# Node degrees of a graph layer from one-hot products with an iota row in SBUF, in place of a second sort and searched key runs

## The chip, the cores and the metric

The kernel runs on one core of a Trainium2 chip. The metric is the device time of one execution in microseconds, the median over the runs shown; lower is better.

## The reference

A block over 16 images of 32x32 pixels and 128 channels: a layer norm and three convolutions with a residual, then a layer norm and a graph-attention router over the 16384 pixels (nodes) with four experts, with a residual again.

```python
h = (x_flat @ W_gat).reshape(M, HEADS, NUM_EXPERTS)          # M = 16384 here, edge_index in [0, 32768)
src, dst = concat(edge_index[0], loops), concat(edge_index[1], loops)      # 524288 edges and loops
e = leaky_relu(a_src[src] + a_dst[dst])
ee = exp(e - segment_max(e, dst)[dst])                        # per destination node
alpha = ee / (segment_sum(ee, dst)[dst] + 1e-16)
agg = segment_sum(h[src] * alpha[:, :, None], dst)            # + b_gat, layer norm, top 2 of 4 experts
out = sum over experts of g * (gelu(x @ W1[ei] + b1[ei]) @ W2[ei] + b2[ei])
```

The edges' numbers run to twice the number of nodes: an edge whose destination lies beyond the last node is dropped, and one whose source lies beyond it reads the last node. So three kinds of edge matter: dropped ones (half), those that read the last node's row, and real ones (a quarter, some 131072), whose source rows have to be fetched one by one.

## The kernel before, in words

Stages. From 0 to some 630 us PE, ACT and DVE run the convolutions and norms, and DVE in between sorts the edges. Each edge is one f32 key that holds destination and source (destination above 14 bits of source); real edges have keys below REAL_END, last-row edges lie between it and VALID_END. The 128x4096 keys stand in SBUF (KA). `sort_row` splits each partition's row so that the small keys come first; the first LROW = 1152 columns of all partitions form list 0, which `sort_keys(0)` sorts over partitions and columns. The next 1152 columns, picked by `pick_rest` (L1285 to L1299), are list 1; what is left is "the rest".

Rows. PE transposes list 0, ACT copies it out (L975), `sources` (L1423) masks the source numbers, and POOL fetches the node rows by indirect DMA: `gather_rows` (L511, the DMA at L519) makes nine gathers of 128 rows a trip, SP stores each trip's rows to `payload`. There are 54 early trips (EARLY_TRIPS), then a loop of catch-up trips whose number is read from a register (`catch_up_trips`, L530 to L534), the rest keys one by one (`fetch_rest`, L546 to L550), four gathers for overlong nodes (L598), and then the main loop: 32 node groups, each with row trips spread over them (61 in all, 540 gathers of L519 in that stage) and gathers of 24 slots per node from `payload` (L616). DVE does the attention of a node group when its slots have landed. PE and ACT run the 32 chunks of the experts (`experts`, L734; 12 layers and 4 groups of transposes a chunk) beside all of this, 16 of them before ACT's exponentials of the last row's start values (init), the others in the main loop.

Starts of the nodes' runs. To know where each node's edges begin in the sorted lists, `find_starts(a)` takes each 64th key as a pivot, compares them with an iota row on DVE (L1471: one-hots of the high and the low part, f32 in, bf16 out, 6 batches of 3 columns per list), PE multiplies the one-hots into a histogram (L773), and POOL gathers key runs of 192 around the starts (`gather_windows`, L566: 32 gathers for list 0 after trip 5, 16 for list 1 after trip 42). DVE counts in each run the keys below each limit (L1523, L1524). For this the sorted keys are stored to DRAM by SP and ACT (`store_keys`), and list 1 has to be sorted fully (`sort_keys(1)`).

Order. Each engine's order is the program's own: POOL's is trips 0 to 4, windows of list 0, trips 5 to 41, windows of list 1, trips 42 to 53, catch-up, rest, main loop. Buffers of two trips of rows alternate (L516 waits for the store of the trip before the last).

```python
for t in range(COLS):                                          # L517, nine a trip
    pool.indirect_dma_start(row_buf[h][:, t, :], None, node_dram, ...)
```

## Time and profile before

| | us |
|---|---|
| median of 3 runs (lowest, highest) | 2872.55 (2868.71, 2882.48) |
| span of the profiled execution | 2297.5 |
| what lies around the span, by the median | 575.05 |
| DVE busy | 1594.7 |
| POOL busy | 1212.5 |
| PE busy | 1086.1 |
| ACT busy | 762.8 |

For the profiled execution only its span is on record, no time of its own. The span runs from the first to the last instruction or transfer. Busy times are of the execution that was profiled; a DMA that an engine issues is not counted as busy, with one exception: POOL's indirect gathers are shown as instructions of POOL, with the time that POOL spends on them. "Issue" stands for idle time that nothing in the profile ends.

### The profile page before, as it was taken

How to read it: one execution, taken by the hardware profiler on the slowest of the kernel's cores; microseconds unless marked ns; L12 is line 12 of the kernel's file. 1: busy time of each engine (PE TensorE's matmuls, PEld its weight loads, DVE VectorE, ACT ScalarE, POOL GpSimd, SP SyncE). 2: the span in 40 equal slices, each digit the busy share in tenths (PEclk: the TensorE clock that was granted, in tenths of full speed). 3: DMA queues.
4: the chain of work that ended last, by engine and by line, in shares of the span. 5: the costliest groups of instructions: out<-in, count | busy, mean ns of one | idle time of the engine just before them, and what ended most of it. 6: DMA issues, size and time to landing. Idle time of an engine off the chain costs nothing. (4 is left out here: it accounts for less than half of the span.)

```text
span 2297.5 us, 16425 instructions
## 1 busy us (share of the span) xinstructions
PE 1086.1 (47%) x4821; PEld 479.8 (21%) x4821; DVE 1594.7 (69%) x3100; ACT 762.8 (33%) x1260; POOL 1212.5 (53%) x1233
## 2 busy tenths in 40 slices
PE   3897878778678887000700102433342425333330
PEld 1233343334533333000300001111111112111110
DVE  6999999995726999999209504364758384747658
ACT  4664846535345554000300002222232324222221
POOL 2000000000066777777777764777777777777771
PEclk8898878787589999555855556766676768676665
DMA  8202031021454322111221611344453535363543
GB/s 297 115 1 74 1 8 38 1 8 39 47 57 110 79 71 71 14 15 29 48 41 29 43 16 41 98 144 121 121 176 85 165 92 176 72 187 73 169 113 100
DMA packets 185735, 182.76 MB, mean 80 GB/s; under 512 B 81580, under 2 KB 164462, under 8 KB 176046
## 3 DMA queue, kind: packets, MB, share of 16 engines
q1 hardware_dynamic: 99262, 88.84, 14.4%
q0 software_dynamic: 43936, 47.85, 12.4%
q10 hardware_dynamic: 42448, 45.04, 6.4%
q8 instruction: 38, 0.62, 0.1%
q14 instruction: 51, 0.42, 0.1%
HBM read 105.23 MB, written 76.40 MB: 79 GB/s over the span
## 5 line engine op out<-in xcount | busy, mean ns | idle before, releaser
L519 POOL DMA_INDIRECT KC<-node_dram,KB x1026 | 1018.4, 993 | 938.8 <-DMA node_dram<-node_out 626.3
L740 PE MATMUL hidden_out<-XT,W 128*128 128x512 f32 x512 | 291.3, 675 | 540.8 <-ACT ARENA_A L956 539.9
L745 PE MATMUL hidden_out<-ARENA_A,W 128*128 128x512 f32 x512 | 264.7, 642 | 24.9 <-ACT ARENA_A L956 24.9
L956 ACT ACTIVATE ARENA_A<-hidden_out,b1c 128x512 f32<-128x512 f32 x256 | 174.2, 687 | 294.5 <-PE hidden_out L740 293.9
L740 PEld LDWEIGHTS hidden_out<-XT,W 128*128 128x128 f32 x512 | 97.3, 211 | 689.5 <-ACT ARENA_A L956 570.1
L1523 DVE TENSOR_TENSOR KB<-XG,MB 128x3072 bf16<-128x3072 f32 x20 | 67.1, 3354 | 163.5 <-DMA XG<-rest_dram,win_i 100.7
L1649 DVE TENSOR_SCALAR KB<-MB 128x16 f32<-128x16 f32 (+1 forms) x33 | 5.7, 172 | 238.3 <-DMA KC<-payload,slot_idx 126.8
L1800 DVE SCALAR_TENSOR_TENSOR XG<-XT,KB,XG 128x128 f32<-128x128 f32 x512 | 144.3, 347 | 14.9 <-DMA XT<-ye_dram 11.2
L959 ACT ACTIVATE ARENA_A<-hidden_out,b2c 128x512 f32<-128x512 f32 x128 | 87.9, 687 | 185.5 <-PE hidden_out L745 185.5
L1026 ACT ACTIVATE TA<-KB 128x400 f32<-128x400 f32 x32 | 16.2, 507 | 373.3 <-DVE KB L1656 373.2
L745 PEld LDWEIGHTS hidden_out<-ARENA_A,W 128*128 128x128 f32 x512 | 98.3, 207 | 182.4 <-ACT ARENA_A L956 103.1
L1201 DVE TENSOR_TENSOR KC<-KA 128x576 f32<-128x576 f32 (+2 forms) x126 | 108.2, 859 | 3.2 <-DVE shift L1095 0.2
L752 PE MATMUL Z<-ident,ARENA_A 128*128 128x128 f32 x512 | 76.5, 296 | 64.9 <-ACT ARENA_D L967 39.9
L1202 DVE TENSOR_TENSOR KC<-KA 128x576 f32<-128x576 f32 (+2 forms) x126 | 107.0, 849 | 0.0
L1201 DVE TENSOR_TENSOR KA<-KC 128x576 f32<-128x576 f32 (+2 forms) x112 | 94.2, 841 | 2.8 <-DVE shift L1085 0.2
L773 PE MATMUL MB<-KC 128*128 128x128 bf16 x36 | 4.9, 307 | 188.5 <-DVE KC L1471 188.5
L1202 DVE TENSOR_TENSOR KA<-KC 128x576 f32<-128x576 f32 (+2 forms) x112 | 93.5, 834 | 0.0
L1524 DVE TENSOR_REDUCE KC<-KB 128x16 f32<-128x3072 bf16 x24 | 80.5, 3354 | 0.8
L616 POOL DMA_INDIRECT KC<-payload,slot_idx x64 | 61.2, 956 | 34.8 <-issue 34.8
L752 PEld LDWEIGHTS Z<-ident,ARENA_A 128*128 128x128 f32 x512 | 58.3, 148 | 100.8 <-ACT ARENA_A L959 51.4
L967 ACT ACTIVATE ARENA_D<-Z 128x512 f32<-128x512 f32 x128 | 70.0, 592 | 25.9 <-PE Z L752 25.9
L1661 DVE TENSOR_TENSOR KC<-KC,TA 128x1600 f32<-128x1600 f32 x16 | 29.1, 1821 | 69.5 <-ACT TA L1026 69.5
(401 smaller groups left out, 2232.0 us busy)
## 6 DMA issues: line engine op xcount, KB each, us to landing
ye_dram<-ARENA_D ACTq DMA_DIRECT2D x32, 1024.0 KB, 4.0
XT<-ye_dram SPq DMA_DIRECT2D x32, 1024.0 KB, 13.5
KC<-node_dram,KB POOLq DMA_INDIRECT x1026
payload<-XT SPq DMA_DIRECT2D x1, 11520.0 KB
payload<-KC SPq DMA_DIRECT2D x115, 90.0 KB, 1.8
XG<-x_dram SPq DMA_DIRECT2D x32, 256.0 KB, 11.3
out_dram<-XG ACTq DMA_DIRECT2D x32, 256.0 KB, 3.4
KA<-in_L_ffn_edge_index_dram SPq DMA_DIRECT2D x1, 2048.0 KB, 9.0
```

The lines of the kernel that those rows point to most:

```text
L519: pool.indirect_dma_start(row_buf[h][:, t, :], None, node_dram, bass.IndirectOffsetOnAxis(ap=KB[:, col:col + 1].bitcast(I32), axis=0)).the ...
L740: last = pe.matmul(PF[i % 2][:, :], W1[:, m // 2, (m % 2) * P:(m % 2) * P + P], XT[:, n * CHUNK:(n + 1) * CHUNK], start=True, stop=True)
L745: last = pe.matmul(PF[i % 2][:, :], W2[:, 2 * m + kk, :], HH[:, 2 * m + kk, :], start=kk == 0, stop=kk == 1)
L752: last = pe.transpose(Z[:, t % 2, x_ * C:(x_ + 1) * C], HH[:, 2 * x_, t * P:(t + 1) * P], ident[:, :])
L956: act.activation(HH[:, m, :], PF[i % 2][:, :], ACT.Gelu, bias=b1c[:, m:m + 1]).then_inc(S["hid_out"], 1)
L959: act.activation(HH[:, 2 * m, :], PF[i % 2][:, :], ACT.Identity, bias=b2c[:, m:m + 1]).then_inc(S["hid_out"], 1)
L967: act.activation(YE[n % 2][:, t, :], Z[:, t % 2, :], ACT.Copy).then_inc(S["exp_out"], 1)
L1201: tt(part(dst, at, 0), part(src, at, 0), part(src, at, 1), ALU.max if d else ALU.min)
L1202: last = tt(part(dst, at, 1), part(src, at, 0), part(src, at, 1), ALU.min if d else ALU.max)
L1523: window_link(tt(below, bc(windows[n % WIN_BUFS], 1, shape), bc(limits, 3, shape), ALU.is_lt))
L1524: window_link(red(found[:, :, j:j + PAIR_J].rearrange("p c j -> p j c"), below, AX.X, ALU.add))
L1800: last = stt(tail_x[j][:, t, :], expert[:, t, x_ * C:(x_ + 1) * C], gate[:, at * TPC + t, x_:x_ + 1], tail_x[j][:, t, :], ALU.mult, ALU.add)
```

## The change

The sorted lists are no longer searched. Instead, for every key of list 0 and list 1 DVE makes two one-hot rows, one of the destination's low seven bits (128 wide) and one of its high bits (256 wide for list 0: the lower half are real nodes, the upper half last-row edges; 128 wide for list 1, the upper half alone). PE multiplies them, 128 keys at a time, into one 128x256 count in PSUM (`H`), which then is the degrees of the nodes. So list 1 doesn't have to be sorted. `drop_counted` takes its last-row edges out once they are to be counted; real keys in it, were there any, stay in the rest, which is now all columns behind list 0.

- Gone: pivots, `find_starts`, `count_keys`, `gather_windows` on POOL, `store_keys` on SP and ACT, `sort_keys(1)`, the boundary products on PE.
- `split_digits(a)` (four DVE instructions a list) writes each key's two digits as bf16, each twice, beside each other. `node_iota` is an iota row of 256 in bf16, in SBUF. `one_hots(a)`: 144 batches of HOT = 8 key columns; a batch is two tensor_tensor (is_equal) into one of two buffers, and from the third batch on it waits until PE has read the buffer (`hot_used`).
- `count_nodes` on PE: eight matmuls per batch, 128x256 (list 0) or 128x128 (list 1). Three batches stand ahead of each of the 16 slots (12 layers, 4 transposes) of the FFN chunks 0 to 2 and 5 to 7 (HOT_SLOTS).
- The starts come from the degrees by two products (with a triangular matrix and with ones) and a scan. ACT loads the node rows after chunk 1 and stores the rest after chunk 7.

```diff
+HOT = 8
+HOT_BATCHES = LROW // HOT
-FIRST_TRIPS = 5
-MID_TRIPS = 42
 EARLY_TRIPS = 54
-REST = ROW - LISTS * LROW
+REST = ROW - LROW
+HOT_SLOTS = (3, 3, 3, 0, 0, 3, 3, 3)
+STORE_REST_AFTER = 7
...
-            for trip in range(FIRST_TRIPS):
-                gather_rows(trip)
-            gather_windows(0)
-            for trip in range(FIRST_TRIPS, MID_TRIPS):
-                gather_rows(trip)
-            gather_windows(1)
-            for trip in range(MID_TRIPS, EARLY_TRIPS):
+            for trip in range(EARLY_TRIPS):
                 gather_rows(trip)
...
+            def count_nodes(count):
+                for n in islice(batches, count):
+                    real = n < HOT_BATCHES
+                    pe.wait_ge(S["hot_ready"], n + 1)
+                    for t in range(HOT):
+                        last = pe.matmul(H if real else H[:, P:], hot_p[n % 2][:, t, :],
+                                         hot_l[n % 2][:, t, 0 if real else P:],
+                                         start=n == 0 and t == 0, stop=n == LISTS * HOT_BATCHES - 1 and t == HOT - 1,
+                                         skip_group_check=True)
+                    last.then_inc(S["hot_used"], 1)
...
+            for n, beside in enumerate(HOT_SLOTS):
+                experts(n, beside)
             pe.wait_ge(S["degree_ready"], 1)
+            pe.matmul(TA[0][:, 0:P], before[:, :], degree_t[:, :], start=True, stop=True)
+            pe.matmul(TA[0][:, P:2 * P], ones[:, :], degree_t[:, :], start=True, stop=True).then_inc(S["starts_summed"], 1)
+            experts(len(HOT_SLOTS))
...
-            sorting = [chain(split_keys(), sort_row(), sort_keys(0)), chain(pick_rest(), sort_keys(1))]
+            sorting = [chain(split_keys(), sort_row(), sort_keys()), pick_rest()]
...
+            def split_digits(a):
+                keys = half(KA, a).bitcast(I32)
+                link(ts(digit_i, keys, SRC_BITS, P - 1, ALU.logical_shift_right, ALU.bitwise_and))
+                link(cp(digits_p, bc(digit_i, 2, [P, LROW, 2])))
+                link(ts(digit_i, keys, SRC_BITS + 7, None, ALU.logical_shift_right))
+                link(ts(digits_l, bc(digit_i, 2, [P, LROW, 2]), float(-(KEY_BIAS // P)), None, ALU.add))
+
+            def one_hots(a):
+                pairs = lambda ap: ap.rearrange("p t (n e) -> p t n e", e=2)
+                for b in range(HOT_BATCHES):
+                    n = a * HOT_BATCHES + b
+                    if n >= 2:
+                        dve.wait_ge(S["hot_used"], n - 1)
+                    cols = slice(b * HOT, (b + 1) * HOT)
+                    for hot, digits, low, high in ((hot_p, digits_p, 0, P), (hot_l, digits_l, (0, P)[a], 2 * P)):
+                        shape = [P, HOT, (high - low) // 2, 2]
+                        last = tt(pairs(hot[n % 2][:, :, low:high]),
+                                  bc(node_iota[:, low:high].rearrange("p (n e) -> p n e", e=2), 1, shape),
+                                  bc(digits[:, cols, :], 2, shape), ALU.is_equal)
+                    last.then_inc(S["hot_ready"], 1)
...
+            split_digits(0)
+            one_hots(0)
             sort_steps(ROW, 1)
+            split_digits(1)
+            drop_counted()
+            one_hots(1)
```

How the instructions move, on the engines that wait or are waited for. POOL before, between the first row gathers and the catch-up trips (L519 row gathers, L566 window gathers, L377 the read of the windows' rounds, L368 that of the catch-up trips):

```order
L519 DMA KC<-node_dram,KB 128x20 x45
L377 TENSOR_LOAD counts_i
L377 ISA x2
...
L566 DMA XG<-keys_dram,win_i 128x192 x8
...
L519 DMA KC<-node_dram,KB 128x20 x333
...
L566 DMA XG<-rest_dram,win_i 128x192 x8
...
L519 DMA KC<-node_dram,KB 128x20 x108
L368 TENSOR_LOAD counts_i
```

and the same place now (L470 is the row gather, L485 that of the catch-up trip, L340 the read of its number):

```order
L470 DMA KC<-node_dram,KB 128x20 x486
L340 TENSOR_LOAD counts_i
L340 ISA x2
L512 UNCONDITIONAL_BRANCH
L512 ISA
L481 ISA
L481 COPY src_buf<-KB 128x9
L482 REGISTER_ALU
L485 DMA KC<-node_dram,src_buf 128x20 x9
```

The 48 window gathers and both reads of a round count between row gathers are gone; 486 row gathers follow each other.

DVE after the sort of list 0, before (L1451 to L1456 make the pivots' digits, L1471 the one-hots, L1523 and L1524 count in a window):

```order
L1456 CAST piv_f<-piv_i 128x18
L1423 TENSOR_SCALAR KB<-KB 128x1152
L1460 COPY MB<-thresholds 128x256
L1471 TENSOR_TENSOR KC<-iota_f,piv_f 128x768
L1471 TENSOR_TENSOR KC<-iota_f,piv_f 128x384
...
L1523 TENSOR_TENSOR KB<-XG,MB 128x3072
L1514 ISA
L1524 TENSOR_REDUCE KC<-KB 128x2x8
```

and now (L1322 masks the sources, L1343 to L1346 are the digits, L1359 the one-hots):

```order
L1322 TENSOR_SCALAR KB<-KB 128x1152
L1376 CAST node_iota<-iota_f 128x256
L1343 TENSOR_SCALAR KC<-KA 128x1152
L1344 CAST KB<-KC 128x2304
L1345 TENSOR_SCALAR KC<-KA 128x1152
L1346 TENSOR_SCALAR KB<-KC 128x2304
L1359 TENSOR_TENSOR KC<-node_iota,KB 128x1024
L1359 TENSOR_TENSOR KC<-node_iota,KB 128x2048
L1359 TENSOR_TENSOR ARENA_Y<-node_iota,KB 128x1024
L1359 TENSOR_TENSOR ARENA_Y<-node_iota,KB 128x2048
```

288 such instructions stand for list 0 where 12 stood, and 288 (128x1024 and 128x8x128) for list 1 behind `pick_rest`. On PE the products stand between the FFN's layers; before, they stood in one block ahead of them (L740 and L745 were the layers, L773 the products, L778 to L785 the offsets):

```order
L773 MATMUL MB<-KC 128x128 x6
L773 MATMUL MB<-XG 128x128 x6
L778 MATMUL TA<-hist_tot,before 128x2
L779 MATMUL TA<-hist_tot,ones 128x1
L785 MATMUL TA<-ident,max_deg 1x128
L740 MATMUL hidden_out<-XT,W 128x512 x3
L745 MATMUL hidden_out<-ARENA_A,W 128x512 x2
```

and now (L672 the products, L685 and L690 the layers):

```order
L672 MATMUL MB<-KC 128x256 x8
L672 MATMUL MB<-ARENA_Y 128x256 x8
L672 MATMUL MB<-KC 128x256 x8
L685 MATMUL hidden_out<-XT,W 128x512
L672 MATMUL MB<-ARENA_Y 128x256 x8
L672 MATMUL MB<-KC 128x256 x8
L672 MATMUL MB<-ARENA_Y 128x256 x8
L685 MATMUL hidden_out<-XT,W 128x512
```

So a layer of these chunks stands behind three batches of products, and with them behind DVE's one-hots.

## Rows read from the trace of the kernel before

**Rows 1.** the page's head: the span, then busy us (share of span) and instructions of engines
```profile
span 2297.5 us, 16425 instructions
...
PE 1086.1 (47%) x4821; PEld 479.8 (21%) x4821; DVE 1594.7 (69%) x3100; ACT 762.8 (33%) x1260; POOL 1212.5 (53%) x1233
```

**Rows 2.** POOL's groups: xcount | busy us, mean ns of one | idle us before, releasers
```profile
L519 POOL DMA_INDIRECT KC<-node_dram,KB x1026 | 1018.4, 993 | 938.8 <-DMA node_dram<-node_out 626.3 <-issue 312.2 <-DVE ARENA_Y L1666 0.3
...
L566 POOL DMA_INDIRECT XG<-keys_dram,win_i x24 | 22.8, 948 | 18.3 <-DVEq L1525 11.3 <-issue 7.0
```

**Rows 3.** busy time of all engines (instructions) in two stretches, granted clock, DMA share, GB/s
```profile
639.00:1361.00 722.00, 290.36 (x845) 126.92 (x845) 477.68 (x668) 169.14 (x260) 547.75 (x535) 0.71 0.27 49
1407.00:2228.00 821.00, 317.38 (x764) 135.53 (x764) 481.93 (x1033) 245.12 (x350) 622.62 (x651) 0.69 0.44 124
```

**Rows 4.** POOL's timeline at five places: start us, duration us, instruction [idle before <-releaser]
```profile
639.13 2.18 POOL L519 DMA_INDIRECT KC<-node_dram,KB  x1 [626.29 <-DMA node_dram<-node_out]
...
737.70 0.95 POOL L566 DMA_INDIRECT XG<-keys_dram,win_i  x1 [11.25 <-DVEq L1525]
...
1360.11 0.21 POOL L530 COPY src_buf<-KB 128x9 int32 x1
...
1377.54 0.59 POOL L546 DMA_DIRECT2D rest_key<-rest_dram  x1 [5.44 <-issue]
...
2226.90 0.95 POOL L519 DMA_INDIRECT KC<-node_dram,KB  x1 [0.30 <-issue]
```

**Rows 5.** DVE's timeline where the catch-up counts and the first rest key are
```profile
1306.04 0.14 DVE L1615 CAST counts_i<-counts_f 1x1 int32<-1x1 f32 x1
...
1380.47 0.15 DVE L1682 TENSOR_SCALAR rest_idx<-rest_key 128x1 int32<-128x1 int32 x1 [60.17 <-DMA rest_key<-rest_dram]
```

**Rows 6.** POOL's groups by form, 697 to 823 us, beside the windows' counting on DVE
```profile
L519 POOL DMA_INDIRECT KC<-node_dram,KB x61 | 57.7, 946 | 18.6 <-issue 18.6
```

**Rows 7.** POOL's groups by form, 840 to 1090 us, beside the second list's sort
```profile
L519 POOL DMA_INDIRECT KC<-node_dram,KB x175 | 197.4, 1128 | 53.3 <-issue 53.3
```

**Rows 8.** DVE's and POOL's timelines at 1314 us, long two-input operations
```profile
1314.67 2.29 DVE L1629 TENSOR_TENSOR KB<-last_row,KC 128x2048 f32<-128x2048 f32 x1
...
1315.76 2.02 POOL L519 DMA_INDIRECT KC<-node_dram,KB  x1 [0.31 <-issue]
```

**Rows 9.** the old one-hots: durations by form of their line; DVE's, then POOL's timeline
```profile
L1471 DVE TENSOR_TENSOR KC<-iota_f,piv_f x12: 548/749/958, 632.2 to 1099.0; 128x768 bf16<-128x768 f32 x6, 128x384 bf16<-128x384 f32 x6
...
1095.44 1.42 DVE L1471 TENSOR_TENSOR KC<-iota_f,piv_f 128x768 bf16<-128x768 f32 x2
...
1096.18 1.03 POOL L519 DMA_INDIRECT KC<-node_dram,KB  x1 [0.30 <-issue]
1097.51 1.04 POOL L519 DMA_INDIRECT KC<-node_dram,KB  x1 [0.30 <-issue]
```

**Rows 10.** a bf16 reduction (the page's groups) and a one-source operation (timeline)
```profile
L1524 DVE TENSOR_REDUCE KC<-KB 128x16 f32<-128x3072 bf16 x24 | 80.5, 3354 | 0.8
...
1267.05 1.09 DVE L1438 TENSOR_SCALAR KB<-KA 128x1792 f32<-128x1792 f32 x1
```

**Rows 11.** POOL's group, 823.8 to 838 us, beside pick_rest; DVE's timeline, start and end of halving
```profile
L519 POOL DMA_INDIRECT KC<-node_dram,KB x11 | 11.1, 1013 | 3.4 <-issue 3.4
...
823.83 0.69 DVE L1201 TENSOR_TENSOR KB<-KA 128x512 f32<-128x512 f32 x1
824.44 0.68 DVE L1202 TENSOR_TENSOR KB<-KA 128x512 f32<-128x512 f32 x1
...
858.90 0.29 DVE L1296 COPY KA<-KB 128x256 f32<-128x256 f32 x1
```

**Rows 12.** PE's timeline at the old one-hots; PE in two stretches (busy us, granted clock, DMA)
```profile
633.80 0.80 PE L773 MATMUL MB<-KC 128*128 128x128 bf16 x6 [3.70 <-DVE KC L1471]
...
632.00:642.00 10.00, 4.90 (x36) 0.50 1.77 35
700.00:850.00 150.00, 134.57 (x385) 1.00 0.35 87
```

More of the change, by code:

```diff
@@ L733, in _, with experts @@
             last_chunk()
-            def experts(n):
+            batches = iter(range(LISTS * HOT_BATCHES))
+            def count_nodes(count):
[8 more added lines that the diff above has]
+                    last.then_inc(S["hot_used"], 1)
+            def experts(n, beside=0):
                 done = n * len(LAYERS)
                 for i, (layer, m) in enumerate(LAYERS):
+                    count_nodes(beside)
                     if layer == 1:
@@ L749, in experts @@
                 for t in range(TPC):
+                    count_nodes(beside)
                     pe.wait_ge(S["exp_out"], n * TPC + t + 1)
@@ L802, in _ @@
             pe.transpose(PO[0:1, 3 * P:], hist_tot[:, 1:2], ident[:, :]).then_inc(S["max_deg_t"], 1)
+            for n in range(len(HOT_SLOTS) + 1, FIRST_CHUNKS):
+                experts(n)
             for n in range(FIRST_CHUNKS, FFN_CHUNKS):
@@ L1295, in pick_rest @@
                 assert n == PICK
[L1296 to L1309 removed]
+                link(cp(a[:, 0:2 * n], b[:, 0:2 * n]))
             def row_steps(keys, other, spare):
@@ L1333, in quadrant_step, with sort_keys @@
                 link(stt(keys, copy, -1.0, frm, ALU.mult, ALU.min))
-            def sort_keys(which):
-                keys, copy, other = (half(k, which) for k in (KA, KB, KC))
+            def sort_keys():
+                keys, copy, other = (half(k, 0) for k in (KA, KB, KC))
                 def times_sign(col, frm=keys):
                     link(ts(keys, frm, signs[:, col:col + 1], None, ALU.mult))
-                if which:
-                    yield from row_steps(keys, other, copy)
                 for m in range(1, LEVELS + 1):
                     if m <= 4:
-                        if m > 1 or which:
+                        if m > 1:
                             times_sign(m - 1, other)
@@ L1556, in _ @@
             measure_rest()
+            dve.sem_inc(S["max_deg_ready"], 1)
             dve.wait_ge(S["nodes_in"], 48)
```

313 lines of the change are left out of this document (62 added, 251 removed).

## The prediction

> **What bounds the kernel now.** All sums are made against the profiled execution. Its span is 2297.5 us [rows 1]; the median of the runs is 2872.55 us, so 575.05 us lie around the span, and I carry them over unchanged. A shift of 0.5% is 14.4 us, about what a measurement of this kernel can tell from no change.
>
> I read the busy shares first. They mislead: DVE is busy 69% and POOL only 53% [rows 1]. The groups of POOL's instructions correct this: 1026 row gathers (L519), 993 ns each, with 312.2 us of idle time before them called issue [rows 2]. That is 0.30 us before each gather, and nothing in the trace ends it; so I count 0.95 + 0.30 = 1.25 us per gather as POOL's own time. Counted so, POOL is full: from 1407 to 2228 us it runs 651 instructions in 821 us, and 651 x 1.25 = 814 [rows 3]. POOL's timeline shows the fixed points: the first gather at 639.13 us waits for the conv stage, the 54 early trips end at 1360.11 us, the rest key follows at 1377.54, and the last row gather comes at 2226.90 [rows 4]. Behind that about 70 us of attention are left. The whole span from 639 us on is therefore POOL's queue, and the change acts on its part from 639 to 1360 us.
>
> Everything else has slack there. DVE has the catch-up counts by 1306.2 us, and POOL reads them only at 1360; DVE then idles 60.17 us for the rest key [rows 5]. So DVE, PE and ACT may end up to some 55 us later at no cost; what counts is what DVE does to POOL's gathers.
>
> **What holds a gather.** While DVE runs the window counts (one SBUF input, or a reduction), gathers take 946 ns [rows 6]. Beside the sort they take 1128 ns [rows 7], 1.43 us with the issue time. The long operations tell why: beside a 2.29 us tensor_tensor with two SBUF inputs, a gather takes 2.02 us [rows 8]. It ends some 0.8 us after the next operation has begun. So I read: a gather that starts inside a DVE operation with two SBUF inputs waits until this operation ends, then takes some 0.8 us, and the next is issued 0.30 us later. A gather is released about 1.12 us after the one before at the soonest, and only where an operation ends.
>
> The window between 639.13 and 1360.11 us then adds up: 720.98 us hold 54 x 9 = 486 row gathers and 32 + 16 window gathers, 534 x 1.25 = 668; 11.25 us of waiting for the first windows' count [rows 4]; and 41 us of holding, 31 of them beside the second list's sort (175 x (1.128 - 0.946) = 32, [rows 6, 7]).
>
> **The change part by part.**
> (1) Removed from POOL: 48 window gathers, 60 us, and the wait of 11.25 us. Catch-up, rest and main loop keep their instructions.
> (2) Removed from DVE: the windows' counting and the second list's sort; on POOL this is worth the holding beside the sort, about 31 us. I leave about 14 us of holding in place: pick_rest's halving and the setup of the last row stay, and the measuring of the rest grows from 1792 to 2944 columns.
> (3) Added on DVE: one-hots, 144 batches of two tensor_tensor for each list. Before, one-hots had f32 inputs, and 768 and 384 elements took 0.95 and 0.55 us, one element per cycle [rows 9]. Now inputs and output are bf16 in SBUF, in adjacent pairs. No row shows such an operation. The bounds are one element per cycle, as the bf16 reduction has (3072 in 3.354 us [rows 10]), and two, as a one-source operation has (1792 in 1.094 us [rows 10]). I take two: two f32 inputs pass at one element per cycle, and half as many bytes per element are read now. This is an estimate. A batch of list 0 (1024 and 2048 elements) is then 0.60 + 1.14 = 1.74 us, 251 us in all; of list 1 (1024 and 1024) 1.21 us, 174 us in all.
>
> The Trainium skill ("VectorE: DVE Perf Modes", section "The perf-mode tier table (the rule you actually need)") gives a bf16 tensor_tensor in SBUF two results per cycle, 1224 ns for 2048. Taken as spacing, its figure makes a batch of list 0 1.84 us, and the sum below would be 14 us more, about no change. In the rows a duration stands 0.08 us over the spacing (0.69 and 0.61 [rows 11]), so I keep 1.74; the page is not shown by any row here.
>
> (4) What this does to POOL. With list 0 a gather released at the end of the 2048-wide operation is ready 1.12 us later, after the 1024-wide one has ended (0.60), and waits for the next end of a wide one: one gather per batch, 1.74 us. The row for this pattern is the old pair of 768 and 384: one gather per pair, 1.04 + 0.30 = 1.34 us, the pair's own period [rows 9]. So 144 x (1.74 - 1.25) = **+71 us**. The bounds are 0 (nothing is held) and +85: 6% over the lock, as the sort's 1.43 us stands over two of its 576-wide operations (0.61 us of spacing at 512 [rows 11], 64 columns more at 1.04 ns, so 1.35 for two).
> With list 1 the operations end every 0.60 us, as the 512-wide ones of pick_rest do. Beside those a gather takes 1.013 + 0.31 = 1.32 us [rows 11]. So 144 x 0.07 = **+10 us**; bounds 0 and +56 (first rival).
> (5) The sum: 486 x 1.2515 = 608.2, the first gather 1.2 longer, +71, +10, +14: 704.4 us. The early trips end at 639.1 + 704.4 = 1343.5 instead of 1360.1: **17 us earlier, 2856 us**.
> (6) What must stay hidden. DVE: one-hots from 641 us, list 0 done at 892; pick_rest's halving took 823.83 to 859.2, 35 us [rows 11], digits and dropping 8 more: 936; list 1 at 1.25 us a batch until 1116; starts and counts some 27 us, so by 1145, 200 us before POOL asks. PE: six 128-column matmuls took 0.80 us at clock 0.50 [rows 12]; eight of 256 columns are then at most 2.13 us at that level and 1.07 at clock 1.00, which the FFN stretch had [rows 12]. It ran 385 instructions in 150 us, 48 a chunk, so 18.7 us a chunk and 1.17 a slot. Three batches and a slot are 3 x 1.07 + 1.17 = 4.4 us, less than DVE's 5.2: PE keeps up. Eight chunks remain after the lists, 150 us: ACT reaches its init exponentials at about 1270 and DVE ends that work by 1300, 43 us before POOL's early end. The removed key stores of SP and ACT free nothing on POOL: only the removed window gathers read them. The larger store of the rest (1.5 MB) goes out at about 1110, 250 us before its reader.
>
> **The rivals.**
> *A, slower: list 1 holds for three operations.* Two operations last 1.21 us, and an undisturbed gather comes back after 1.25. If it then finds the third operation running by more than some 0.05 us, it waits for its end: 1.82 us instead of 1.25. In 178 us 98 gathers fit, 98 x 0.57 = +56 instead of +10: **2902 us**. It decides against the change once the holding in list 1 passes 27 us. For it: the sort's mean of 1.43 lies above two of its operations (1.35), so some of its gathers took three. Against: the 512-wide rows, of nearly the same spacing, show 1.32 in the mean.
> *B: one element per cycle.* Batches of 3.34 and 2.27 us: lists done at 641 + 481 + 44 + 327 = 1493, init after eight chunks at 1655. The rest key then waits until 1668 instead of 1377: **3163 us**. For it speaks the bf16 reduction.
> *C: 16-bit inputs don't hold gathers.* POOL is through at 1262, and the rest key waits for DVE's init at 1298: 79 us earlier, **2793 us**. For it: gathers beside one-input and reduction rows aren't held; against: the two inputs are still both in SBUF.
> *D: PE stays at the low level (1.2 GHz).* Three batches and a slot: 3 x 2.13 + 2.3 = 8.7 us in list 0, 5.5 in list 1: lists done at 1368, init at 1540, **about 3010 us**. Against: the stretch that had PE busy 90% was granted 1.00 [rows 12].
> *E: DVE is held as POOL is.* Each operation would wait for a whole gather: 3.64 and 3.11 us a batch, lists done at 1656, **about 3340 us**. Against: DVE's 512-wide operations kept a spacing of 0.61 us beside gathers [rows 11]. The Trainium skill ("SBUF — State Buffer", section "Who interferes with whom") says that a DVE instruction with two SBUF inputs contends with a GpSimd instruction that reads SBUF, and that the one that issues first holds the ports while the other fully blocks. The trace agrees for the gather (2.02 us [rows 8]), not for DVE.
> That the change did not do what it says (real keys left to the rest loop) I give nothing: that loop ran one trip before [rows 4], so the second list held no real key.
>
> **How the numbers follow.** The forecast of 2856 with its spread of some 15 us: 0.56, of which 0.32 lies below 2858 and 0.24 within 14 us of no change. A: 0.20 (0.03 of it within). C: 0.10. B and D: 0.06 each. E: 0.02. Faster by over 0.5%: 0.32 + 0.10 = 0.42; within: 0.27; slower: 0.17 + 0.14 = 0.31. The likeliest case's own range is 2835 to 2875. The range takes in C (2793) and A (2902) with their spread, 2790 to 2910, and leaves out B, D and E, 0.14, and some of the tails.
>
> **What would show it.** Right: no POOL wait between 639 and the catch-up trip; L470 gathers at 1.74 us spacing while L1359 runs 2048-wide, at 1.25 to 1.32 in list 1; the rest key at about 1361; DVE idle before it by 40 us or more. Wrong: L1359 1024-wide over 0.75 us (B); gathers at 0.95 throughout (C); PE's clock at 0.50 from 641 to 892, and DVE waiting for hot_used (D); gathers of 1.5 us in list 1 (A); POOL idle before the rest key by more than 6 us, which would mean that the FFN chunks have become the bound.

## The result, and the profile after

| us | before | with the change |
|---|---|---|
| median of five runs | 2874.22 | 2947.64 |
| lowest, highest | 2868.71, 2882.48 | 2932.92, 2953.82 (four runs) |
| ratio, with its 95% interval | | 1.0242 (1.0211 to 1.0272) |

The change makes the kernel slower by 2.4%, some 70 us. Of its five runs, the one that was profiled took 3088.51 us, 4.6% above the next; it counts in the median but not in the range and the ratio, and the rows of the change below are from another profiled execution, of 2948.21 us. Beside it the kernel before was profiled a second time, in an execution of 2879.56 us. The heads of both pages, the change first:

```profile
span 2946.6 us, 20726 instructions
...
PE 1376.0 (47%) x7034; PEld 655.7 (22%) x7034; DVE 1610.9 (55%) x3152; ACT 765.7 (26%) x1260; POOL 1214.0 (41%) x1184
```

```profile
span 2877.6 us, 16425 instructions
...
PE 1230.1 (43%) x4821; PEld 511.6 (18%) x4821; DVE 1589.6 (55%) x3100; ACT 765.8 (27%) x1260; POOL 1196.5 (42%) x1233
```

These two heads already contradict the frame of the prediction. The time of these executions is the span plus 1.6 and 2.0 us (2948.21 - 2946.6, 2879.56 - 2877.6), and in all the other profiled runs with a time 1.6 to 2.3 us. Nothing of 575 us lies around the span. The execution of [rows 1], with a span of 2297.5 us, was one that none of the timed runs resembles: in the second profile of before the missing time is inside the span, 251 us of it ahead of the four gathers for overlong nodes (they start at 1652.80 instead of 1401.84 us) and 329 us in the main loop behind them. So the profile of before to compare with is the second one, and in it POOL's timeline has two long waits that [rows 4] doesn't have (columns: start us, duration us, instruction, idle before and its releaser):

```profile
1402.23 0.94 POOL L566 DMA_INDIRECT XG<-rest_dram,win_i  x1 [213.57 <-issue]
...
1607.79 0.19 POOL L530 COPY src_buf<-KB 128x9 int32 x1 [49.06 <-issue]
...
1652.80 0.94 POOL L598 DMA_INDIRECT KA<-payload,extra_idx  x1 [19.43 <-DVE extra_idx L1723]
```

POOL waits 213.57 us for the second list's windows (the last gather of trip 41 ends at 1188.7), and 49.06 us for the catch-up counts. The same view of the change:

```profile
1341.28 0.96 POOL L470 DMA_INDIRECT KC<-node_dram,KB  x1 [0.30 <-issue]
...
1565.54 0.64 POOL L481 COPY src_buf<-KB 128x9 int32 x1 [223.30 <-issue]
...
1706.33 0.58 POOL L497 DMA_DIRECT2D rest_key<-rest_dram  x1 [128.38 <-DVEq L1500]
...
1730.82 0.95 POOL L528 DMA_INDIRECT KA<-payload,extra_idx  x1 [19.42 <-DVE extra_idx L1553]
```

The early trips end at 1342.2 us, as forecast (1343.5). But then POOL stands still for 223.30 us until DVE has the counts, and for 128.38 us until the rest key may be read. The four gathers ahead of the main loop start at 1730.82 instead of 1652.80 us, 78 us later. What follows takes 1215.8 us (2946.6 - 1730.8), against 1224.8 before. So the main loop gives back 9 us, and 78 - 9 = 69 us is the difference of the two spans. The waits before the main loop are 89 us longer (223.3 + 128.4 against 213.6 + 49.1); POOL's own work there is 11 us shorter.

**What makes the waits.** PE's rows by stretch show it (us, busy us and instructions, granted clock, DMA share, GB/s). The change:

```profile
700.00:850.00 150.00, 101.73 (x687) 0.95 0.34 37
930.00:1130.00 200.00, 40.61 (x82) 0.53 0.14 27
...
1220.00:1380.00 160.00, 18.90 (x114) 0.52 0.08 12
```

The second profile of before:

```profile
700.00:850.00 150.00, 36.99 (x56) 0.53 0.22 45
...
1220.00:1380.00 160.00, 144.59 (x407) 1.00 0.13 55
```

In [rows 12] PE ran 385 instructions from 700 to 850 us at clock 1.00. In the second profile of the same kernel it runs 56 in that stretch, at clock 0.53, near the low level of 1.2 GHz. It comes to full speed only between 1220 and 1380 us, which is when POOL waits for its windows. In the change it is the other way round: PE works from 700 to 850 us, when list 0's one-hots hold the gathers to one in 1.74 us, and nearly stands still until the trips are through. A chunk of the FFN took 18.7 us in [rows 12]; read from ACT's stores of the chunks' results, it took 119 to 135 us in the first stretch of before (ends at 727, 846, 981 and 1115 us), and some 19 us in the wait (ten ends from 1218 to 1388).

ACT's timeline in the change, from 1000 us on, and POOL's beside it:

```profile
1004.16 0.69 ACT L875 ACTIVATE ARENA_A<-hidden_out,b1c 128x512 f32<-128x512 f32 x1 [4.91 <-PE hidden_out L690]
1014.66 0.69 ACT L878 ACTIVATE ARENA_A<-hidden_out,b2c 128x512 f32<-128x512 f32 x1 [9.81 <-issue]
1020.26 0.69 ACT L875 ACTIVATE ARENA_A<-hidden_out,b1c 128x512 f32<-128x512 f32 x1 [4.91 <-remote]
...
1037.06 0.69 ACT L878 ACTIVATE ARENA_A<-hidden_out,b2c 128x512 f32<-128x512 f32 x1 [9.82 <-remote]
```

```profile
1002.50 0.94 POOL L470 DMA_INDIRECT KC<-node_dram,KB  x1 [0.30 <-issue]
1003.75 0.94 POOL L470 DMA_INDIRECT KC<-node_dram,KB  x1 [0.30 <-issue]
```

and PE's:

```profile
999.30 3.78 PE L690 MATMUL hidden_out<-ARENA_A,W 128*128 128x512 f32 x4 [3.52 <-ACT ARENA_A L875]
1004.90 1.13 PE L685 MATMUL hidden_out<-XT,W 128*128 128x512 f32 x2 [1.82 <-ACT ARENA_A L875]
1015.40 2.08 PE L685 MATMUL hidden_out<-XT,W 128*128 128x512 f32 x2 [9.37 <-ACT ARENA_A L878]
1021.00 3.47 PE L690 MATMUL hidden_out<-ARENA_A,W 128*128 128x512 f32 x4 [3.52 <-issue]
```

L878 of ACT reads what L690 of PE made, and L875 what L685 made. The four products of L690 that start at 999.30 us end at 1003.08 by the profile; ACT needs them and nothing else, and starts at 1014.66, 11.6 us later. The two of 1004.90 end at 1006.03, and ACT's next start is at 1020.26, 14.2 us later. In the other direction nothing is late: ACT ends at 1015.35, and PE, which may be one layer ahead, starts at 1015.40. Where the trace has a record of PE's addition to the semaphore, it stands just ahead of ACT's start (1020.24 for 1020.26, 1037.04 for 1037.06). So the delay is on PE's side, while POOL sends a gather every 1.25 us. Without it, in the run with a slower POOL that is read below, the same pair looks so (its line numbers are nine higher; four products end at 1201.91, ACT starts at 1201.95):

```profile
1200.03 1.88 PE L699 MATMUL hidden_out<-ARENA_A,W 128*128 128x512 f32 x4
1201.95 0.69 ACT L887 ACTIVATE ARENA_A<-hidden_out,b2c 128x512 f32<-128x512 f32 x1 [1.03 <-PE hidden_out L699]
```

The ends of matmuls are modelled in the profile; so these rows alone don't tell a late signal from a late end of the product. The distances do. Ahead of each ACT start stand two of PE's instructions (L685) or four (L690 and the transposes). ACT's starts from 1004.16 to 1042.66 us are 10.5, 5.6, 6.3, 10.5 and 5.6 us apart: the long ones for four instructions, the short ones for two, 38.5 us for 14 in all. Beside the counts of list 1, DVE waits for batches of eight and ACT for 26 (three batches and a layer's two):

```profile
1143.46 1.29 DVE L1359 TENSOR_TENSOR ARENA_Y<-node_iota,KB 128x1024 bf16<-128x1024 bf16 x2 [21.08 <-remote]
1165.86 1.36 DVE L1359 TENSOR_TENSOR KC<-node_iota,KB 128x1024 bf16<-128x1024 bf16 x2 [21.11 <-remote]
1193.86 1.29 DVE L1359 TENSOR_TENSOR ARENA_Y<-node_iota,KB 128x1024 bf16<-128x1024 bf16 x2 [26.64 <-issue]
```

```profile
1172.16 0.69 ACT L875 ACTIVATE ARENA_A<-hidden_out,b1c 128x512 f32<-128x512 f32 x1 [72.90 <-remote]
1244.96 0.69 ACT L875 ACTIVATE ARENA_A<-hidden_out,b1c 128x512 f32<-128x512 f32 x1 [72.11 <-remote]
```

That is 22.4 us for eight, 28.0 for ten and 72.8 for 26: 2.8 us an instruction each time, for products of 128x128 in bf16 as for 128x512 in f32. A chunk has 48, which makes 134.4 us, and two of the chunks of before took just that (846.3 to 980.7 and on to 1115.1). A signal that is late by itself would not be later with more instructions ahead of it. So beside these gathers PE's instructions count as done at a pace of one in 2.8 us, where a chunk at full speed has one in 0.39 (18.7 / 48). The recorded starts and modelled ends don't show it, and what holds PE no run shows. "Late signals" below means this slow pace.

### The profile page after: what moved, and what is told of

Its sections match the earlier page's. It is cut to its first block, busy times and chain, and to the rows that moved or that the text cites. A ratio compares the mean times of both kernels' runs of the same rounds, so it can differ in the third digit from the quotient of the medians.

```text
span 3086.9 us, 20726 instructions
## 1 busy us (share of the span) xinstructions
PE 1397.2 (45%) x7034; PEld 665.7 (22%) x7034; DVE 1611.6 (52%) x3152; ACT 766.1 (25%) x1260; POOL 1190.5 (39%) x1184
## 4 chain that ended last, share of the span: by engine, by line
DVE 40%; another core or an unknown queue 28%; PE 15%; issue 8%; ACT 6%; ACTq 1%; DMA 1%; SPq 1%; POOL 0%; DVEq 0%; POOLq 0%
PE hidden_out L690 7%; DVE ARENA_Y L1359 6%; DVE KC L1359 6%; DVE XG L1630 5%; PE hidden_out L685 4%; DVE KC L1119 2%; DVE KC L1118 2%; DVE KA L1118 2%; DVE KA L1119 2%; ACT ARENA_A L875 2%; PE MB L672 1%; DVE ARENA_Y L1497 1%; ACT ARENA_A L878 1%; ACT ARENA_D L886 1%
## 5 line engine op out<-in xcount | busy, mean ns | idle before, releaser
L470 POOL DMA_INDIRECT KC<-node_dram,KB x1026 | 1042.7, 1016 | 940.0 <-DMA node_dram<-node_out 626.9
L685 PE MATMUL hidden_out<-XT,W 128*128 128x512 f32 x512 | 321.3, 730 | 673.7 <-ACT ARENA_A L875 524.0
L1359 DVE TENSOR_TENSOR KC<-node_iota,KB 128x1024 bf16<-128x1024 bf16 (+1 forms) x288 | 223.7, 817 | 283.4 <-remote 245.8
L1359 DVE TENSOR_TENSOR ARENA_Y<-node_iota,KB 128x1024 bf16<-128x1024 bf16 (+1 forms) x288 | 223.6, 817 | 280.0 <-remote 259.9
L875 ACT ACTIVATE ARENA_A<-hidden_out,b1c 128x512 f32<-128x512 f32 x256 | 174.7, 687 | 732.4 <-remote 413.5
L690 PE MATMUL hidden_out<-ARENA_A,W 128*128 128x512 f32 x512 | 304.3, 725 | 87.9 <-ACT ARENA_A L875 57.0
L672 PE MATMUL MB<-KC 128*128 128x256 bf16 (+1 forms) x1152 | 133.3, 263 | 351.9 <-issue 216.4
L685 PEld LDWEIGHTS hidden_out<-XT,W 128*128 128x128 f32 x512 | 101.5, 228 | 820.7 <-ACT ARENA_A L875 566.4
L672 PE MATMUL MB<-ARENA_Y 128*128 128x256 bf16 (+1 forms) x1152 | 133.1, 263 | 280.3 <-issue 230.6
L878 ACT ACTIVATE ARENA_A<-hidden_out,b2c 128x512 f32<-128x512 f32 x128 | 88.0, 687 | 614.6 <-remote 373.1
L672 PEld LDWEIGHTS MB<-KC 128*128 128x128 bf16 x1152 | 90.6, 103 | 413.1 <-issue 239.1
L672 PEld LDWEIGHTS MB<-ARENA_Y 128*128 128x128 bf16 x1152 | 91.1, 103 | 339.2 <-issue 245.6
L690 PEld LDWEIGHTS hidden_out<-ARENA_A,W 128*128 128x128 f32 x512 | 107.0, 228 | 259.8 <-issue 131.1
L546 POOL DMA_INDIRECT KA<-payload,slot_idx x64 | 60.6, 948 | 164.8 <-DVE ARENA_Y L1497 139.7
L1492 DVE TENSOR_TENSOR KA<-KA,TA 128x1600 f32<-128x1600 f32 x17 | 31.0, 1822 | 153.0 <-ACT TA L943 113.0
```

The source lines that it names most:

```text
L546: pool.indirect_dma_start(slot_rows[h][:, t, 0:SLOTS, :].rearrange("p k w -> p (k w)"), None, listed, bass.IndirectOffsetOnAxis(ap=slot_id ...
L672: last = pe.matmul(H if real else H[:, P:], hot_p[n % 2][:, t, :], hot_l[n % 2][:, t, 0 if real else P:], start=n == 0 and t == 0, stop=n ...
L685: last = pe.matmul(PF[i % 2][:, :], W1[:, m // 2, (m % 2) * P:(m % 2) * P + P], XT[:, n * CHUNK:(n + 1) * CHUNK], start=True, stop=True)
L690: last = pe.matmul(PF[i % 2][:, :], W2[:, 2 * m + kk, :], HH[:, 2 * m + kk, :], start=kk == 0, stop=kk == 1)
L875: act.activation(HH[:, m, :], PF[i % 2][:, :], ACT.Gelu, bias=b1c[:, m:m + 1]).then_inc(S["hid_out"], 1)
L878: act.activation(HH[:, 2 * m, :], PF[i % 2][:, :], ACT.Identity, bias=b2c[:, m:m + 1]).then_inc(S["hid_out"], 1)
```

## The experiments

**The theories.** The one that the traces suggest is called E in the texts on record (it is not rival E of the prediction): beside gathers that follow each other at 1.25 us, PE's signals reach ACT and DVE late (those texts take the signal itself to be late); where gathers come more slowly or POOL stands still, they are in time. The kernel before had a pause for PE, POOL's wait for windows, and the change removes this pause. Its rivals: the three loads of node rows that ACT issues behind chunk 1 set the lateness off (theory A of the first three texts); or (F) the chunks are slow for a reason of PE's own, such as its low clock after idling, which slower gathers would not lift; later, that it is the number of additions to semaphores.

### Both kernels again, and the node loads moved

The first two runs have no edit. The third issues the loads of the node rows on ACT behind chunk 16 instead of chunk 1:

```diff
             evacuate_keys()
-            feed_forward(1)
+            feed_forward(STORE_REST_AFTER)
+            store_rest()
+            feed_forward(FIRST_CHUNKS - STORE_REST_AFTER)
             act.wait_ge(S["node_stored"], 16 * GROUPS)
...
-            feed_forward(STORE_REST_AFTER - 1)
-            store_rest()
-            feed_forward(FIRST_CHUNKS - STORE_REST_AFTER)
```

> The kernel before, unchanged, to see whether the profiled span of 2297.5 us and the timed 2872 us belong together. Theory A (in the trace of the change, what PE adds to a semaphore reaches DVE and ACT 10 to 40 us late, and the kernel before has the same in its timed runs, after its own node loads at 1280 us): a span of about 2870 us, with the early trips still ended near 1360 us and the extra 570 us in the main loop, as waits of ACT on PE. Theory B (575 us lie around the span, and only the change has late semaphores): a span of 2297 us and a time near 2872 us.

> The change, unchanged, for a profile of an execution near 2945 us. Theory A: smooth one-hot batches of 1.74 us from 641 us until the node loads of ACT are issued (after FFN chunk 1, near 735 us), then batches of 20 us and more while POOL gathers. Theory B: the slow batches begin somewhere else, with no tie to the loads.

> The change with ACT's three node loads (with the 16-byte packets) moved from behind FFN chunk 1 to behind chunk 16. Theory A, loads as the trigger: list 0 at 1.74 us a batch until 892 us, list 1 done near 1120 us, early trips end near 1343 us, and a time of 2840 to 2870 us. Theory B, where gathers slow the exchange between DVE and PE whatever ACT loads: batches of 20 us as before, and a time within 1% of the change's 2945 us.

Measured: before 2879.56 us, the change 2948.21 us, both read above. Before's span of 2877.6 us is that of theory A, but 251 of the missing us lie ahead of the main loop, not all within it; and in the change the one-hots stay smooth beyond the loads behind chunk 1 (725 us), to the end of list 0 at 908 us. With the loads moved 2993.62 us (2981.31 to 3002.89), 1.0417 of before (1.0364 to 1.047), against 2875.51 us for before on that chip. POOL's timeline there:

```profile
1727.87 0.65 POOL L481 COPY src_buf<-KB 128x9 int32 x1 [384.10 <-issue]
...
1773.96 0.94 POOL L528 DMA_INDIRECT KA<-payload,extra_idx  x1 [19.43 <-DVE extra_idx L1552]
```

The early trips end at 1343.8 us, the chunks end as late as in the change (the fifth at 1078 us, the sixth at 1418, against 1099 and 1418), and the counts now wait for the loads behind the 16 chunks as well. So the loads don't set it off.

### Slower gathers

POOL gets a small memset behind row gathers, into a tile that nobody reads. Each memset has to end before the next one starts. (The diff is that of "all"; "early" has `if trip < EARLY_TRIPS:`.) The number is its columns; "early" puts it behind the 486 gathers of the early trips, "all" behind all 1026 row gathers, and "before" is the kernel before with the same edit. Nothing of the computation is left out.

```diff
                     ).then_inc(rows_gathered[h], 16)
+                    if True:
+                        if pads[0]:
+                            pool.wait_ge(S["padded"], pads[0])
+                        pool.memset(pad_tile[:, 0:PAD], 0.0).then_inc(S["padded"], 1)
+                        pads[0] += 1
```

> The change with a memset of 128x384 on POOL behind each of the 486 early row gathers (some 0.4 us more per gather, about 1.7 us, the spacing that the one-hots of list 0 gave them). Theory E (PE's signals to ACT and DVE come late only while POOL's gathers follow each other at 1.25 us): they come at once through the whole early stage; the early trips end near 1465 us, POOL does not wait for the catch-up counts, the extra gathers start near 1510 instead of 1731 us, and the time is near 2730 us. Theory F (they come late when PE has little to do, whatever the spacing of the gathers): the chunks stay slow until the early trips end at 1465, the extra gathers start near 1850, and the time is near 3070 us.

> The same memset behind all 1026 row gathers. Theory E: the main loop too runs at POOL's pace, 540 gathers of 1.7 and 128 of 1.25 us and some 70 us behind them, 1150 instead of 1216 us, and the time is near 2660 us. Theory F: the main loop gets longer by up to 200 us, and the time is over 3100 us.

> The same with a memset of 128x128, some 0.2 us per gather, 1.45 us in all. Theory E: if this spacing is wide enough, the early trips end near 1400 us, the extra gathers start near 1440, the main loop takes some 1010 us, and the time is near 2460 us; if it is not, the chunks are as slow as in the change and the time is near 2950 us. Theory F: over 2980 us.

> The kernel before with a memset of 128x384 behind all its row gathers. Theory E: FFN chunks of about 19 us from 641 us on, POOL's own time bounds both stages (534 early gathers of 1.65 us end near 1540), and the time is near 2700 to 2750 us. Theory F: over 2950 us.

Measured: 2725.34 us, 2562.58, 2635.58 and 2602.96, beside 2884.99 for before on this chip. POOL has more to do and the kernel is faster by up to 13% than the change as it stood (2562.58 / 2948.21 = 0.869). The page's groups of the run with 384 columns everywhere (xcount | busy us, mean ns of one | idle us before), and POOL's timeline there:

```profile
L474 POOL DMA_INDIRECT KC<-node_dram,KB x1026 | 1054.1, 1027 | 799.4 <-DMA node_dram<-node_out 625.8
...
L481 POOL MEMSET pad_tile<- 128x384 f32 x1026 | 446.7, 435 | 0.6
```

```profile
1301.03 0.95 POOL L474 DMA_INDIRECT KC<-node_dram,KB  x1 [0.16 <-issue]
1301.98 0.44 POOL L481 MEMSET pad_tile<- 128x384 f32 x1
1302.58 0.95 POOL L474 DMA_INDIRECT KC<-node_dram,KB  x1 [0.17 <-issue]
```

A gather every 1.55 us: the memset lasts 0.44 us, but 0.13 of the gap before the next gather goes (0.30 to 0.17). PE in the same stretches as above:

```profile
930.00:1130.00 200.00, 143.18 (x1294) 0.98 0.16 41
1150.00:1280.00 130.00, 116.68 (x335) 1.00 0.24 70
```

1294 instructions where the change had 82, and 335 in 130 us afterwards, which is [rows 12]'s rate (385 in 150): 48 a chunk, 18.6 us. The clock went up with it. So F falls: a slower POOL alone brings PE to full speed. List 1's counts and all 16 chunks are done by 1288 us, as step 6 had worked them out (1270), and POOL finds the counts and the rest key ready. With "early" alone the main loop keeps its late signals; it starts at 1506.19 us, and 1506.2 with the change's main loop of 1215.8 makes a span of 2722.0, where 2723.6 was measured. 384 columns everywhere and before with 384 came out some 100 us below what was expected: the main loop too had been losing time to late signals, more than I had counted. 128 columns (1.34 us, not the 1.45 that the text on record took) came out between the two cases: from 1209 to 1418 us a chunk takes 68 to 71 us, 1.4 us an instruction, half the delay. So a memset behind each gather doesn't remove the lateness by being there; its length counts.

### How slow, and what it is that counts

Two runs give other lengths of memset. One puts a trip's nine memsets behind its nine gathers. One adds, to the kernel with 384 columns, 100 additions by SP a trip to semaphores that nobody waits for.

```diff
# trip384
+                for t in range(COLS):
...
+                    pool.memset(pad_tile[:, 0:PAD], 0.0).then_inc(S["padded"], 1)
...
# events, on SP
+                for _ in range(EVENTS):
+                    sp.sem_inc(S[f"unheard{h}"], 1)
```

> The change with a memset of 128x256 behind every row gather; by the memsets before (0.22 us at 128 columns, 0.435 at 384) one of 0.33 us, so gathers 1.45 us apart, between 1.34 (signals of PE partly late) and 1.55 (not late). Theory E with the limit below 1.45: POOL's pace bounds both stages, 0.1 us less for some 880 gathers than with 384, near 2480 us. With the limit above 1.45: between 2563 and 2636 us, with POOL waiting for DVE in the main loop.

> The same with 128x320, 1.50 us apart. Theory E: some 2520 us if its signals are in time, and if they are late here already, no better than the 2563 us at 1.55.

> The 1026 memsets of 128x384 in groups of nine behind each trip's nine gathers instead of one behind each gather: the same gathers per trip time, but at 1.25 us within it. If the limit is on the mean over some 10 us and more: a time near the 2563 us of the spread memsets. If it is on what comes within a few us: PE's signals are late for 11 of each 15 us, chunks and main loop are slower, and the time is 2650 us or more.

> The kernel with 384 columns, and SP adds 100 times to a semaphore that nobody reads, ahead of its wait for each trip. A gather adds to semaphores 16 times, 9.4 to 10.3 per us at this spacing; this is some 7 per us more on average. If it is the number of semaphore additions that makes PE's signals late: chunks slow down again, and the time is 2800 us or more. If it is the gathers' own traffic: near 2563 us.

Measured: 2477.01 us, 2517.66, 2759.00 and 2562.81, beside 2864.54 for before. 256 and 320 columns (1.45 and 1.50 us) are as expected. POOL's timeline with the nine memsets of a trip together:

```profile
1245.38 0.95 POOL L474 DMA_INDIRECT KC<-node_dram,KB  x1 [0.16 <-issue]
...
1256.32 4.23 POOL L481 MEMSET pad_tile<- 128x384 f32 x9
1260.71 0.95 POOL L474 DMA_INDIRECT KC<-node_dram,KB  x1 [0.16 <-issue]
```

A trip takes 15.33 us (1260.71 - 1245.38) instead of nine times 1.55 = 13.95: set apart, a memset costs its whole length. On 114 trips that makes 114 x 1.38 = 157 of the 196 us by which the run is longer (2759.00 - 2562.58). Lateness is nearly gone all the same: the last eight chunks of the early stage end 19 us apart (1211 to 1344), although nine gathers in a row stand at 1.25 us; the second and third chunk with list 1's counts take 76 and 79 us there instead of 61. So a pause in each 15 us does nearly what one behind each gather does. By the time alone (2650 us or more) the text on record would read a limit on what comes within a few us; the chunks speak against it. Some 39 us of the longer time are not accounted for. The distance of gathers alone doesn't decide either: from 1130 to 1343 us the change runs 155 gathers, 1.37 us apart in the mean, and PE is at 2.8 us an instruction, where 128 columns at 1.34 had 1.4. The additions do nothing:

```profile
span 2561.2 us, 33151 instructions
```

11,400 instructions more, and the span of 2561.0 us without them. The number of additions that engines make is not it. What of a gather's own traffic is, stays open; no run has gathers without their additions to a semaphore. Another rival stays open as well, the recording of the profile: the trace of [rows 1] has 27612 additions to semaphores on record, the second one of the same kernel 8271, that of the same kernel with 384 columns 24697. So most are missing where PE is slow (many elsewhere too: 14602 with 256 columns); whether the recording takes part in the slowness or suffers from the same thing, no run shows.

### The limit, and both kernels without the lateness

> The change with 256 columns behind every row gather again, timed in rounds. Theory E: 2477 us within 0.5%, a ratio to the kernel before near 0.862.

> The kernel before with the same memset behind its row gathers, timed in rounds: what the change is worth where PE's signals are in time. POOL bounds both then. Between the two stand the 48 window gathers (60 us), the waits for windows (about 10 and 11 us) and the holding beside the second sort against the holding beside the one-hots of both lists: from the pair with 384 columns (2603 and 2563) the change is worth 40 us, so near 2517 us here. If signals are late in one of the two at this spacing, the pair differs by 80 us or more.

> The change with 192 columns, gathers 1.40 us apart. Theory E: some 2440 us if the limit lies below this spacing; if above, PE's signals come late here and there, POOL waits for DVE in the main loop, and the time is 2480 to 2600 us.

> The change with 320 columns behind every row gather (1.50 us apart), timed in rounds. Theory E: 2518 us within 0.5%, no wait of POOL for DVE in the main loop.

> The kernel before with the same memset, timed in rounds. Both kernels are bound by POOL then; the change is worth the 48 window gathers (60 us) and the waits for windows (20 us) less what the one-hots hold more than the sort did: by the pair with 384 columns 40 us, so near 2558 us. If the change were worth nothing by itself, the two times are equal within 0.5%.

The last kernel takes 256 columns in the early trips and 320 in the main loop:

```diff
+PAD, EARLY_PAD = 320, 256
...
+                        pool.memset(pad_tile[:, 0:EARLY_PAD if trip < EARLY_TRIPS else PAD], 0.0).then_inc(S["padded"], 1)
```

> The change with 256 columns in the early trips, where 1.45 us were wide enough in both runs at 256, and 320 in the main loop, where they were not always. The early stage of the one (extra gathers from 1478 us) and the main loop of the other (1027 us from there on): 2507 us.

Each ratio is to the kernel before on the same chip; the runs with 256 and 192 columns here are of one chip, those with 320 and the mixed one of another.

| behind each row gather | the change, us | ratio to before | before with it, us | ratio to before |
|---|---|---|---|---|
| nothing | 2947.64 | 1.0242 (1.0211 to 1.0272) | 2874.22 | |
| 192 columns, 1.40 us (one run) | 2631.94 | | | |
| 256 columns, 1.45 us | 2527.55 (2517.58 to 2537.51) | 0.8766 (0.8733 to 0.8799) | 2532.69 (2532.34 to 2550.12) | 0.8816 (0.8782 to 0.8849) |
| 320 columns, 1.50 us | 2518.60 (2517.42 to 2521.81) | 0.8762 (0.8731 to 0.8794) | 2540.20 (2537.14 to 2540.66) | 0.8833 (0.8802 to 0.8864) |
| 256 early, 320 in the main loop | 2507.91 (2507.06 to 2509.01) | 0.8725 (0.8695 to 0.8756) | | |

256 columns missed: 2477 us in the earlier single run, 2517.58 to 2537.51 here, on another chip. In its profile POOL waits 16 to 21 us at 1829, 2081 and 2335 us in the main loop, which the earlier one doesn't have. So at 1.45 us the lateness is gone in some executions and not in others, in the main loop; whether that goes by the execution or by the chip is not shown. 192 columns are late again, and longer than the 2480 to 2600 us expected. The pair at 256 columns was to differ by 40 us and differs by 5; with the change still late in part there, it says little. At 320 columns the runs agree within 0.2%, and the pair came out at half of the 40 us expected. The mixed version, as expected (2507), is faster than both kernels, by 12.75% against before.

At 320 columns the signals are in time in both kernels, and the change is faster by 2540.20 - 2518.60 = 21.6 us, 0.85%; the gathers ahead of the main loop start at 1489.2 instead of 1512.0 us. Without the lateness the loss of 70 us is gone, and this is what the change is worth at this spacing. Its terms are not those of the 17 us forecast: list 0's batch of 1.74 us costs a gather 0.24 us over 1.50, where it was 0.49 over 1.25, and beside list 1 gathers come 1.81 us apart, 0.31 over 1.50.

## Why the prediction was wrong, and where it was right

**What failed first is the frame**, the first paragraph: "575.05 us lie around the span, and I carry them over unchanged". A remainder of a fifth of the time, on one core, was a sign that the profiled execution was unlike the timed ones. Everything that was then argued from slack (POOL full, DVE 60 us early [rows 5]) describes an execution in which PE's signals came in time, and no timed one is like it. Why that one was free of lateness at 1.25 us a gather [rows 6] stays open; no run shows it a second time.

**Step 6 failed on that ground**: "Three batches and a slot are 3 x 1.07 + 1.17 = 4.4 us, less than DVE's 5.2: PE keeps up". Beside gathers at 1.25 us in the timed kind of execution, three batches of list 1, half as wide as those of the sum, and a slot took 72.8 us: 26 instructions of 2.8. With it fell DVE done "by 1145, 200 us before POOL asks" and "43 us before POOL's early end", and the prediction's own sign of being wrong came: POOL idle ahead of the rest key, because the chunks had become the bound. Beside list 0 step 6 held: PE ran 687 instructions from 700 to 850 us at clock 0.95. Behind it, with gathers at 1.25 to 1.40 us, the chunk after 1099 us ended at 1418. DVE's longest wait for PE's products is in the change's waits (us in total, times, longest us), with POOL's and ACT's:

```profile
ACT ARENA_A L875 <- remote: 329.4, 28, 72.9
...
POOL src_buf L481 <- issue: 223.3, 1, 223.3
...
DVE KC L1359 <- remote: 196.6, 4, 134.7
...
POOL rest_key L497 <- DVEq L1500: 128.4, 1, 128.4
```

List 1 was counted at 1538 instead of 1116 us, and the eight chunks ahead of the init exponentials followed from 1540 to 1693. When both ran, PE was at full speed, with POOL standing still:

```profile
1560.00:1700.00 140.00, 118.95 (x339) 0.99 0.15 62
1420.00:1540.00 120.00, 85.59 (x850) 1.00 0.06 26
```

That is the 352 us of POOL's two waits. The sum did hold step 6 once the gathers were slowed to 1.55 us: 1288 us for the 16th chunk, against 1270.

**The removed wait was not free.** The 11.25 us of [rows 4] were counted as gain; the timed executions had 213.57 us for the second list's windows, and these were the stretch ahead of the main loop in which PE ran at full speed, with ten of the 16 chunks in it. The change takes away a wait of POOL, and with it what others did in that time. The lists' counts need PE where they come beside gathers, so the wait came back, later and longer.

**Right: the sum on POOL's queue** (steps 1 to 5). The early trips end at 1342.2 us; 1343.5 was forecast. Step 3's two elements per cycle, from DVE's timeline in the change at 700 us, with POOL's beside it:

```profile
699.79 1.22 DVE L1359 TENSOR_TENSOR ARENA_Y<-node_iota,KB 128x2048 bf16<-128x2048 bf16 x1
700.92 1.82 DVE L1359 TENSOR_TENSOR KC<-node_iota,KB 128x1024 bf16<-128x1024 bf16 x2
```

```profile
700.38 1.44 POOL L470 DMA_INDIRECT KC<-node_dram,KB  x1 [0.30 <-issue]
702.13 1.43 POOL L470 DMA_INDIRECT KC<-node_dram,KB  x1 [0.31 <-issue]
```

2048 elements last 1.22 us, and batches start 1.74 us apart (step 3: 1.74). The Trainium skill ("VectorE: DVE Perf Modes", section "The perf-mode tier table (the rule you actually need)") gives 1224 ns for this operation: the duration agrees, and the spacing stays under it, as the prediction chose. Step 4's one gather per batch is in POOL's rows: 1.43 to 1.44 us each, one every 1.74. From 930 to 1343 us the 313 gathers took 1008 ns in the mean, 1.32 with the gap, as step 4 took for list 1. That agreement is luck: most of list 1 ran only later, beside no gather, and gathers of 0.94 and of 1.09 us stand side by side at 1204 to 1212 us, where DVE is idle; what made some of them longer, no run shows.

**The rivals.** B falls with the 1.22 us, and C with the held gathers. A was not put to the test in the change, where list 1 hardly met a gather. In the run with 384 columns it did, from a spacing of 1.55 us, and there its mechanism came: a gather each 1.81 us, three operations of 0.60.

```profile
1022.92 1.21 POOL L474 DMA_INDIRECT KC<-node_dram,KB  x1 [0.16 <-issue]
...
1024.73 1.21 POOL L474 DMA_INDIRECT KC<-node_dram,KB  x1 [0.16 <-issue]
```

So the +10 us for list 1 stays unproven at 1.25 us. E falls: DVE kept its batch of 1.74 us while gathers ran. The Trainium skill's rule ("SBUF — State Buffer", section "Who interferes with whom"), that the one that issues first holds the ports while the other blocks, is met by the trace in one direction alone: the gather waits, DVE doesn't. D named the right engine and the low clock, with a price far too small: by D a batch takes 2.13 us at 1.2 GHz, and 22.4 were measured, for one half as wide. The clock of 0.53 stands beside a PE that is busy 40.61 of 200 us (930 to 1130); beside list 0 it was granted 0.95. None of the rivals was the mechanism, and the time came out above all but those of B, D and E.

## What to carry to other kernels

Set the time of a profiled execution against its span before anything else; where a large remainder is left, the profile may be of an execution unlike the timed ones, and it has to be taken again before any slack is read from it. A wait that a change removes may be the only time in which another engine gets its work done: ask who works in it. Where an engine's recorded ends look fine and the engines behind it start late, set the distances of those starts against the number of instructions in between. Where a queue of back-to-back gathers runs beside a chain of short steps from one engine to the next, a small pause behind each gather is worth a try: here, with 320 columns, it cost 0.25 us on each of 1026 gathers and made the two kernels 12% and 15% faster.

## What the runs showed of the hardware that was not expected

- Beside indirect gathers at 1.25 us each, in every profiled execution but that of [rows 1], ACT and DVE see PE's instructions done at one in some 2.8 us, small or large; with a memset of 128 columns behind each gather (1.34 us) at one in 1.4; with 320 columns (1.50 us) ACT starts 0.04 us behind PE's modelled end, in the median. With 256 (1.45 us) the early stage is in time and the main loop not always. 100 more additions to semaphores a trip change nothing (2562.81 against 2562.58 us). From ACT to PE nothing is late (0.05 us).
- A memset of 384 columns directly behind a gather lasts 0.44 us and costs 0.30, since the next gather's gap shrinks from 0.30 to 0.17 us; behind the last of nine it costs its whole length.
- With the pauses that make POOL busier, PE's clock goes up from 0.53 to 0.98 in the stretch from 930 to 1130 us, in which PE runs 1294 instructions instead of 82.
